# Value rows projected in the group that uses them, in a five-pass graph transformer on one core

## What is computed

```python
x = _layernorm(x + _L0_gnn_ref(x, adj, adj, Wq, Wk, Wv, bv, Wo, bo))
x = _layernorm(x + _L1_gnn_ref(x, adj, Wq, bq, Wk, bk, Wv, bv, beta))
x = _layernorm(x + _L2_gnn_ref(x, adj, Wl, bl, Ws, bs, Wr, br, ln_w, ln_b))
x = _layernorm(x + _L3_gnn_ref(x, adj, Wq, Wk, Wv, bv, Wo, bo))

# layers 0 and 3 (layer 1: no Wo, q and k with biases, softmax over the edges only)
q = (x @ Wq.T).reshape(b, n, 12, 32)          # k likewise, v with + bv
scores = jnp.einsum('bqhd,bkhd->bhqk', q, k) * scale + bias
p = softmax(scores, axis=-1)
out = jnp.einsum('bhqk,bkhd->bqhd', p, v).reshape(b, n, 384) @ Wo.T + bo

# layer 2, two rounds of
a = softmax(h @ h.T / sqrt(384)); attn = a * adj / (sum(a * adj) + 1e-10)
ctx = (attn * upper) @ (h @ wl.T + bl) + diag(attn) * (h @ ws.T + bs) + (attn * lower) @ (h @ wr.T + br)
h = relu(layernorm(ctx) * g + beta)
```

## Time and profile before

| | |
|---|---|
| median of three runs | 2626.3 us (2626.18 to 2629.85) |
| profiled execution, its time | 2625.92 us |
| its span | 2624.2 us |
| mean granted clock of TensorE | 0.975 |
| TensorE busy | 2445.8 us (93%) |
| VectorE busy | 1966.2 us (75%) |
| POOL busy | 1966.9 us (75%) |
| ACT busy | 1605.0 us (61%) |

### The profile page before, as it was taken

The page is one execution under the profiler, slowest core; times in us unless marked ns, Lnnn a source line. Parts: engine busy times, 40 slices in busy tenths (PEclk is TensorE's granted clock), DMA queues, the critical chain, the costliest instruction groups (busy, mean ns, idle before and its releaser), DMA issues. The chain is left out here.

```text
span 2624.2 us, 64888 instructions
## 1 busy us (share of the span) xinstructions
PE 2445.8 (93%) x21554; PEld 2097.4 (80%) x21554; DVE 1966.2 (75%) x3543; ACT 1605.0 (61%) x3414; POOL 1966.9 (75%) x2127
## 2 busy tenths in 40 slices
PE   6999999996999999959999998999997999999997
PEld 5888888885877777748888887888886888888886
DVE  4777788785788888877777776776765677777876
ACT  4667666664666556634544554766665666766665
POOL 4888888884677777765566566999996778888886
PEclk9999999997999999969999998999998999999998
DMA  7222232223433333316323316434343222223211
GB/s 138 67 67 70 69 75 69 59 62 70 85 77 79 79 76 79 80 55 114 72 63 73 70 49 127 102 93 104 90 105 83 51 68 68 70 68 73 61 46 52
DMA packets 320602, 200.71 MB, mean 76 GB/s; under 512 B 243426, under 2 KB 320484, under 8 KB 320484
## 3 DMA queue, kind: packets, MB, share of 16 engines
q1 hardware_dynamic: 317028, 197.93, 32.3%
q10 hardware_dynamic: 3456, 1.28, 0.3%
HBM read 136.22 MB, written 62.91 MB: 76 GB/s over the span
## 5 line engine op out<-in xcount | busy, mean ns | idle before, releaser
L491 PE MATMUL l_ps_p<-xT,w 128*128 128x512 f32 x2304 | 593.7, 404 | 59.1 <-PEq L1588 15.1
L491 PEld LDWEIGHTS l_ps_p<-xT,w 128*128 128x128 f32 x2304 | 425.2, 191 | 154.3 <-issue 39.1
L431 POOL TENSOR_TENSOR l_pr<-l_sc,l_st 128x768 f32<-128x768 f32 x192 | 286.4, 1492 | 176.9 <-DVE l_st L826 176.9
L1353 ACT ACTIVATE l_hlr<-l_ps_h 64x384 f32<-64x384 f32 x512 | 248.8, 486 | 250.1 <-PE l_ps_h L1273 241.4
L836 DVE TENSOR_REDUCE l_st<-l_pr 128x12 f32<-128x768 f32 x192 | 182.8, 952 | 244.3 <-ACT l_pr L703 244.3
L385 POOL TENSOR_TENSOR v<-v,l_bvs 128x768 f32<-128x768 f32 x192 | 359.7, 1873 | 0.0
L1199 POOL TENSOR_TENSOR l_hlr<-l_hlr,l_sides 128x768 f32<-128x768 f32 x128 | 235.8, 1842 | 133.1 <-ACT l_hlr L1353 129.5
L1273 PE MATMUL l_ps_h<-second,xT 128*128 128x384 f32 x1728 | 332.2, 342 | 0.0
L1273 PE MATMUL l_ps_h<-w,xT 128*128 128x384 f32 x1728 | 324.7, 342 | 0.0
L1273 PEld LDWEIGHTS l_ps_h<-second,xT 128*128 128x128 f32 x1728 | 300.1, 189 | 29.8 <-issue 28.7
L1273 PEld LDWEIGHTS l_ps_h<-w,xT 128*128 128x128 f32 x1728 | 299.5, 189 | 29.8 <-issue 27.5
(11 more groups left out here) (144 smaller groups left out, 4577.5 us busy)
## 6 DMA issues: line engine op xcount, KB each, us to landing
rows<-l_yo SPq DMA_DIRECT2D x256, 192.0 KB, 1.9
xa<-rows SPq DMA_DIRECT2D x256, 192.0 KB, 4.2
l_xr<-rows SPq DMA_DIRECT2D x192, 192.0 KB, 2.4
l_xr<-in_x SPq DMA_DIRECT2D x64, 192.0 KB, 2.4
out<-l_yo SPq DMA_DIRECT2D x64, 192.0 KB, 1.9
xa<-in_x SPq DMA_DIRECT2D x62, 192.0 KB, 4.2
l_edge<-in_adj SPq DMA_DIRECT2D x80, 128.0 KB, 2.3
raw<-in_L_gnn_Wk SPq DMA_DIRECT2D x12, 144.0 KB, 6.6
```

The source lines that it names most:

```text
L431: nc.gpsimd.tensor_tensor(pr[b][:, :, :], sc[b][:, :, :], st[b][:, 0, :].unsqueeze(2).to_broadcast([P, HEADS, NODES]), ALU.subtract).then_ ...
L491: last = nc.tensor.matmul(bank[:, :], W[m][:, l, t, o * P:(o + 1) * P], rows[:, r, t, :], start=c + t == 0, stop=c == 2 and t == KT - 1)
L1353: i = nc.scalar.activation(hlr[b][half * NODES:(half + 1) * NODES, g, :], ps_h[m][g * NODES:(g + 1) * NODES, :D], ACT.Copy)
```

## The change

**Projections.** The values move to the front of the table, and a group's values are now made in that group itself; queries and keys are still for the next one. Units 0 and 1 have two value projections each, unit 2 the three queries, unit 3 the three keys. Ahead of a pass only the six pieces of queries and keys are made; the last group makes its own four values.

```diff
-        AHEAD = (("q", 0), ("q", 1), ("q", 2), ("k", 0), ("k", 1), ("k", 2), ("v", 0), ("v", 1), ("v", 2), ("v", 3))
-        BETWEEN = (((), (0,), (1,)), ((), (2,), (3,)), ((4,), (5,), (6,)), ((7,), (8,), (9,)))
+        AHEAD = (("v", 0), ("v", 1), ("v", 2), ("v", 3), ("q", 0), ("q", 1), ("q", 2), ("k", 0), ("k", 1), ("k", 2))
+        BETWEEN = (((), (0,), (1,)), ((2,), (), (3,)), ((4,), (5,), (6,)), ((7,), (8,), (9,)))
+        AT_FIRST = range(4, len(AHEAD))
-        def exists(i):
-            return inside(i + 1, groups)
+        def exists(i, pos):
+            return inside(i if AHEAD[pos][0] == "v" else i + 1, groups)
...
+                rows = xT[par] if kind == "v" else xT[1 - par]
...
-            for pos in range(len(AHEAD)):
-                if pos in (0, 3, 6):
-                    pe.wait_ge(dve_w, wb + pos + KT)
+            for pos in AT_FIRST:
                 ahead(-1, 1, pos)
...
+                    if s == 0:
+                        pe.wait_ge(dve_w, wb + steps)
+                        if isinstance(i, int) and i < 2:
+                            pe.wait_ge(act_first, i + 1)
+                        else:
+                            pe.wait_ge(act_k2[par], pair)
                     scores(n, par, s)
```

**Weights of the next pass** are turned two at a time over the last six units instead of in the last group, in layer 1 through two tiles in SBUF instead of PSUM banks:

```diff
+        wt = [a.sb(f"wt{b}", [P, D]) for b in range(2)] if nxt and nxt.turned else None
+        def steps_at(i, s, later):
+            if not nxt or not isinstance(i, int):
+                return ()
+            return tuple(j for j in range(steps) if units - 6 + j // 2 + later == i * UNITS + s)
...
-                            for step in range(KT * (s - 1), KT * s):
-                                weight_low(nxt, step, next_bank(step))
+                    for step in steps_at(i, s, 1):
+                        weight_low(nxt, step, wt and wt[step % 2])
```

```diff
-            for b in range(2):
-                sp.wait_ge(s_out[b], 16 * (units // 2))
+            if nxt is None:
+                for b in range(2):
+                    sp.wait_ge(s_out[b], out_base + 16 * (units // 2))
```

**Layer 2, second round.** The tenth matmul and what prepared it go. VectorE adds the bias (`own`) to the projection, and multiplies by the diagonal and adds the context in one operation, as in the first round:

```diff
-                if ends and m == SELF:
-                    if isinstance(n, int) and n == 0:
-                        pe.wait_ge(c_row, 3)
-                    last = nc.tensor.matmul(ps_h[m][:, :D], pick[:, :], bias[:, :], start=False, stop=True)
...
-                    nc.vector.tensor_tensor(c0[b][:, :], ps_c[:, :D], hs[b][:, :], ALU.add).then_inc(dve_c, 1)
-                else:
-                    nc.vector.scalar_tensor_tensor(out=c0[b][:, :], in0=hs[b][:, :], scalar=diag[gpar][:, s:s + 1],
-                                                   in1=ps_c[:, :D], op0=ALU.mult, op1=ALU.add).then_inc(dve_c, 1)
+                nc.vector.scalar_tensor_tensor(out=c0[b][:, :], in0=hs[b][:, :], scalar=diag[gpar][:, s:s + 1],
+                                               in1=ps_c[:, :D], op0=ALU.mult, op1=ALU.add).then_inc(dve_c, 1)
```

More of the change, by code:

```diff
@@ L242, in attention_pass @@
         ln = [a.sb(f"ln{b}", [P, 12]) for b in range(2)]
-        yo = [a.sb(f"yo{b}", [P, D]) for b in range(2)]
+        yo, s_out = shared.yo, shared.s_out
+        out_base = 16 * (units // 2) * me.k
         ps_s = a.ps("ps_s", [P, 2 * 512])
@@ L415, in _ @@
                     nc.gpsimd.memset(v2[g][:, :, :, :], 0.0).then_inc(shared.c_v2, 1)
-                for t in range(KT):
+                for t in range(KT - g):
                     rows_low(g, g, t)
@@ L680, in _ @@
                 act.wait_ge(dve_kb, 2)
-            for pos in range(len(AHEAD)):
-                if me.k == 0 and pos == 6:
-                    act.wait_ge(shared.c_v2, 2)
+            for pos in AT_FIRST:
                 ahead(-1, 1, pos)
-                if pos in (2, 3, 4):
-                    rows_high(1, 1, pos - 2)
+                if pos in (6, 7, 8):
+                    rows_high(1, 1, pos - 6)
             if wo:
@@ L978, in digcn_pass @@
         loaded = list(shared.loads)
-        own = None if ends else a.sb("own", [P, D])
-        if ends:
-            pick = shared.pick
-            brow = a.sb("brow", [P, D])
-            bround = a.sb("bround", [P, D], F32R)
-            bias = a.sb("bias", [P, D], F32R)
-            c_zero, c_row = a.sem("c_zero"), a.sem("c_row")
+        own = a.sb("own", [P, D])
         sides = a.sb("sides", [P, GPU, D])
@@ L1028, in digcn_pass @@
         s_xr = [a.sem(f"s_xr{b}") for b in range(2)]
-        s_out = [a.sem(f"s_out{b}") for b in range(2)]
         s_small, c_mask, c_held = a.sem("s_small"), a.sem("c_mask"), a.sem("c_held")
@@ L1041, in digcn_pass @@
                                "pool_nb2"))
-        n_small = (2 if ends else 1) + 4 + 2
-        taken = 3 if ends else 2
+        n_small = 1 + 4 + 2
+        taken = 2
         steps = 3 * KT
@@ L1072, in _ @@
             sp.dma_start(edge[0][:, :, :], adj_g[0]).then_inc(s_edge[0], 16)
-            if ends:
-                for row in (0, 32):
-                    sp.dma_start(brow[row:row + 1, :], row_biases[SELF]).then_inc(s_small, 16)
-            else:
-                sp.dma_start(own[:, :], row_biases[SELF].to_broadcast([P, D])).then_inc(s_small, 16)
+            for b in range(2):
+                sp.wait_ge(s_out[b], out_base)
+            sp.dma_start(own[:, :], row_biases[SELF].to_broadcast([P, D])).then_inc(s_small, 16)
             for g in range(GPU):
@@ L1265, in project @@
                     pe.wait_ge(dve_w, wb + KT * (m + 1))
-                if m == SELF and not ends:
+                if m == SELF:
                     if counted(n):
@@ L1489, in itself @@
             def itself(n, b):
-                if ends or not inside(n, units):
+                if not inside(n, units):
                     return
```

144 lines of the change are left out of this document (63 added, 81 removed).

## The result

The changed kernel takes 2779.0 us (median of four runs, 2775.4 to 2780.4); the kernel before, on the same chip, takes 2626.2. The ratio is 1.058, with a 95% interval of 1.056 to 1.059. The forecast was 2679 with a range of 2632 to 2712: the direction was right, the size was not. The profiled execution has a span of 2776.7 us, 152.5 more than before.

What follows compares the result with a forecast made beforehand. TensorE's list of instructions was taken to bound layers 0 and 3, so new waits are paid in full. From 2625.9 us, +76 for waits, +11 for the clock and -34 for savings gave 2679, range 2632 to 2712.

Steps and rivals of the forecast that it cites:

- The seam in layers 0 and 3: Between groups, TensorE waits for ACT's copy of k2 before the next scores: about 1.5 us per group, upper bound 2.0.
- Units 0 and 1: Layers 0 and 3: unit 1's output projection waits 1.8 us for VectorE's L869 instead of 0.56, +1.2 per group.
- exp's delay: Unit 0, layers 0 and 3: ACT copies v0 ahead of exp, so exp starts 0.3 us later.
- L841's shortening: VectorE's chain to L869: L841 takes 0.4 us instead of 0.97 beside POOL's value bias, so the chain wins 0.55.
- The two waits together: Layers 0 and 3: seam and unit 1 waits add 2.7 us per group (2.5 to 3.8), +76 us over 28 groups.
- The clock: Layers 0 and 3: the clock falls behind new waits in one group of four, 1.6 us each, +11 us (0 to 45).
- the clock falls in most groups: Rival for layers 0 and 3: clock loss of 45 us, giving 2713 us; chance 0.13.
- Layer 1: Its steady state: the wait on k2 replaces TensorE's waits for VectorE's scores, so 0 (-5 to +20).
- The savings: Starts, ends and layer 2: pass starts -20.2, bias matmuls -11.8, rounded bias -2, stores -6, weights -1.6 and +3.5.
- The waits are absorbed: Rival: layers 0 and 3 keep 36.0 us per group and only the savings are left, 2592 us; chance 0.18.
- Only the seam is paid: Rival: L869 comes as much earlier as TensorE does, leaving 28 x 1.5 - 34, 2634 us; chance 0.13.
- Layer 1 pays too: Rival: one more us in each of layer 1's 14 groups, 2693 us; chance 0.10.

Runs made afterwards that it cites:

- experiment 1: Changed kernel with the k2 projection moved ahead of unit 3's output projection in layers 0 and 3: 2703.0 us, ratio 1.028 to the kernel before.
- experiment 6: Changed kernel with all ten projections again made for the next group in the old order, all else as after the change: 2645.1 us, ratio 1.007.
- experiment 4: Changed kernel with ACT doing exp ahead of v0's copies in unit 0 of all three attention layers: 2780.7 us, ratio 1.058.
- 2: Changed kernel with v3, the fourth value projection, moved ahead of unit 1's output projection in layers 0 and 3: 2707.7 us, ratio 1.030.
- 7: Changed kernel with exp ahead of v0's copies in all attention layers and, in layers 0 and 3, POOL's value bias last in the unit: 2697.2 us, ratio 1.027.
- Experiment 5: Changed kernel with ACT copying k1 ahead of exp instead of behind it in unit 3 of layer 1: 2751.6 us, ratio 1.047.
- experiment 9: Changed kernel with all projections again for the next group in the old order, and rows made in their old places: 2616.7 us, ratio 0.9964.

## Why the forecast was wrong, step by step

**The seam in layers 0 and 3** was right: 1.5 us forecast, 1.45 measured, paid in each of the 28 groups and won back whole when k2 had 1.6 us of work behind it (experiment 1).

**Units 0 and 1** was right in place and too small: a wait of 1.8 us forecast, 2.21 measured, +1.65 per group instead of +1.2. The mis-sized terms are exp's delay (0.5 us, not 0.3) and L841's shortening, which I had credited with 0.55. It did shrink, from 0.97 to 0.18, but the third operation of the chain grew from 0.17 to 0.76 beside POOL, so that 0.2 was left. By the duration of 0.97 taken as it stood, the wait would have been 2.35, nearer to the truth than the 1.8 that I worked out with the port lock. The rule of the Trainium skill (SBUF - State Buffer, "Who interferes with whom") is not refuted, since L874 again ended with POOL's operation (277.45 + 0.76 = 278.21 against 277.17 + 1.00 = 278.17). What failed is that I applied it to one instruction and not to the ones behind it. The two waits together were forecast at 2.7 per group and are 3.1. A misreading cost nothing: the 36.02 us that I took for every group are those of the shorter ones. The groups of before alternate between 36.0 and 36.5, and in the longer TensorE also waits 0.3 us for POOL's L440.

**The clock** failed. "I charge one group in four" was 11 us, for 7 falls; the clock fell in 23 groups, 36 us. The case was a rival ("the clock falls in most groups") with 0.13. I had compared each new wait by itself with one wait ahead of a prologue's value block, behind which the clock held. One wait that held is a poor witness: in layer 1 of experiment 6 the clock held once behind 2.70 us and fell once behind 1.82. What the runs show is how often it fell in the 28 groups, by TensorE's waits in one group: with 1.45 and 2.21 in 23; with 1.45, 0.5 and 1.77 in 25 (experiment 4, in a few groups with 1.45 and 1.67); with about 1.9 alone in 3 (experiment 1); with 1.45 and 0.6, or 1.45 and 0.9, in none (2 and 7). So the length of the longest wait alone does not tell it, and a second wait in the group made a fall likelier; in experiment 4 that was the seam's, together with the short one for POOL, and the two were not parted.

**Layer 1** is the step that failed most: "the wait on k2 takes the place of those, so 0 (-5 to +20)". Measured are +60.5 us, 4.1 per steady group. Two things were missed. First, the wait's length: I carried 1.5 us over from layers 0 and 3, but in layer 1 exp, k1's copies and the rows stand ahead of k2's on ACT, and it is 3.55. The order of ACT's instructions in unit 3 and the wait of exp for POOL were both to be had from the order listing and the trace of before; I listed ACT's order only for unit 0. Second, the clock. The waits that were to be replaced are 2.1 us per group:

```profile
PE l_ps_p L491 <- DVE l_sc L819: 13.6, 15, 1.0
PE l_ps_p L491 <- ACT l_qT L639: 9.1, 10, 1.0
```

Half of them are for VectorE's scores, as I had it; the others are for ACT's copies of queries (9.1 us of 26 in the window 700 to 1100) and values, which I had not looked at. Against these 2.1 it now has 3.55 and, still for VectorE's scores, 1.04, and 1.5 us of clock: +4.0. Experiment 5 shows the first, since the order of two operations on ACT alone won 27.8 us in layer 1, 12 of them through the clock. That layer 1 is held by the move at all is shown by experiment 9, where it is at 465.1 us without it.

**The savings** were right in most: -31 us measured at the starts, ends and in layer 2, against -38 in the table. Layer 0's start gave 7.0 of 8.7; layer 0's end and layer 3's last group came within about 2 us. The stretch with layer 2 gave 16.5 of 21, and the starts of TensorE's instructions say where it fell short. Layer 3's start gave 5.9 of 6.5. The second round, from its first projection to layer 3's first, is 6.7 us shorter (420.9 instead of 427.6), where I had 13.8 for the bias matmuls and the wait for the rounded bias. The matmuls did give 0.17 us per unit. The first context did come 5.6 us sooner behind the round's first projection (8.5 instead of 14.1), but two units later TensorE stands 5.3 us for POOL:

```profile
1717.77 1.55 PE L1300 MATMUL l_ps_c<-l_hlr,l_aT 128*64 128x384 f32 x4 [5.34 <-POOL l_hlr L1211]
```

With the clock low behind it (the 27 matmuls of 4.98 us take 6.08) and some smaller waits, eight units at the round's start take 9 us longer than eight in its middle, so that the 2 us taken as won there, and more, were lost again. Layer 1's end made up for a part: 3.6 us shorter, where I had it longer.

**The other rivals.** "The waits are absorbed" is out: TensorE's new waits were paid in full where they arose, and when one was taken away it did not come back elsewhere (1 and 2). "Only the seam is paid" is out as well. "Layer 1 pays too" was true at four times its price.

**What stays open.** By what rule the clock falls. The counts above point to the wait at the seam as having a part in it, but do not say why it held in 5 of 28 groups of the changed kernel, fell in 3 of 28 without the seam's wait, and held behind 2.70 us where it had fallen behind 1.82.
